# A Mamba-style scan and a mixture of experts on one core: large SBUF tiles moved to multiples of 128 bytes, and the last residual add shared between GpSimd and VectorE

## What is computed

```python
x = x + layernorm(scan(layernorm(x)))      # selective state-space scan, 512 channels x 16 states
x = x + layernorm(moe(layernorm(x)))       # mixture of experts
```

## The kernel before

| tiles | stage | before | changed |
|---|---|---|---|
| `ident` | all | 0 | 0 |
| `xnT` | prepare | 96 | 64 |
| `xpT`, `a_u`, `a_w1`, `a_low`, `a_lg`, `a_dt`, `a_dx` | prepare | 0 | 96 |
| `Bt`, `Ct`, `dts`, `dtxs`, `w1_*`, `w2_*`, `u`, `pr` | mix | 32 | 0 |
| `Xh`, `Xl`, `hhs`, `hls` | mix | 96 | 0 |
| `Xbh`, `Xbl`, `hh`, `hl`, `h32`, `raw`, `xrow`, `yst` | experts | 32 | 0 |
| `Xah`, `Xal`, `Xch`, `Xcl`, `W1h`, `W1l`, `W2h`, `W2l` | experts | 96 | 0 |
| `d_x1*`, `d_y*` | experts, end | 96 | 0 |

## Time and profile before

### The profile page before, as it was taken

One profiled execution on the slowest core, in us unless ns is written; L12 is line 12 of the kernel. 1 busy time (PEld: TensorE's weight loads), 2 busy tenths in 40 slices (PEclk: granted clock), 3 DMA queues, 4 the chain that ended last, 5 costly groups with the idle time before them and its releaser, 6 DMA issues.

```text
span 3578.8 us, 43069 instructions
## 1 busy us (share of the span) xinstructions
PE 3174.4 (89%) x15191; PEld 2574.6 (72%) x15191; DVE 1854.1 (52%) x2708; ACT 1425.5 (40%) x2529; POOL 1732.0 (48%) x1577
## 2 busy tenths in 40 slices
PE   6455699998999987989999999999999999999992
PEld 3233577777777775778888888888888888888881
DVE  6698989998899880552332233222222322222225
ACT  7554676676766762311221322312213213222113
POOL 1187787987888863531440532513415326235102
PEclk8655799999999998979999999999999999999996
DMA  8859688696796946810330421312303214123026
GB/s 258 249 169 243 176 228 221 195 270 185 225 235 201 257 134 183 247 58 19 77 75 9 106 51 42 100 21 71 77 12 98 59 27 109 27 59 83 16 77 229
DMA packets 276920, 463.42 MB, mean 129 GB/s; under 512 B 32065, under 2 KB 107729, under 8 KB 276706
## 3 DMA queue, kind: packets, MB, share of 16 engines
q1 hardware_dynamic: 206656, 266.21, 26.1%
q0 software_dynamic: 68288, 194.06, 20.8%
q10 hardware_dynamic: 1762, 0.40, 0.1%
HBM read 363.44 MB, written 97.14 MB: 129 GB/s over the span
## 4 chain that ended last, share of the span: by engine, by line
PE 55%; DVE 2%; DMA 1%; issue 1%; POOL 1%; ACT 1%; SPq 0%; POOLq 0%; DVEq 0%; ACTq 0%
PE c_psH L1769 27%; PE c_psY L1813 26%; PE c_psT L1760 1%; PE c_psT L1864 1%; DVE d_y L1740 1%; DVE d_st L1724 1%; PE c_psY L1809 0%; DVE yst L1536 0%; DMA xrow<-x_d 0%; DMA raw<-in_w 0%; POOL W1l L1406 0%; DVE hh L1546 0%; ACT h L1320 0%; POOL W2l L1406 0%; DMA acc_d<-yst,sidx 0%
## 5 line engine op out<-in xcount | busy, mean ns | idle before, releaser
L1552 DVE CAST hh<-h 128x512 fp32r<-128x512 f32 (+1 forms) x400 | 176.9, 442 | 1282.3 <-ACT h L1326 1256.5
L826 POOL TENSOR_TENSOR u<-dtxs,Bt 128x512 f32<-128x512 f32 x512 | 670.8, 1348 | 164.2 <-DVE b_psA L729 147.1
L1326 ACT ACTIVATE h<-c_psH,b1e 128x512 f32<-128x512 f32 (+1 forms) x384 | 236.7, 616 | 1281.6 <-PE c_psH L1769 1263.0
L729 DVE TENSOR_TENSOR_SCAN b_psA<-b_psA,carry,u 128x512 f32<-128x512 f32 x512 | 657.0, 1283 | 59.8 <-ACT b_psA L599 56.7
L1813 PE MATMUL c_psY<-W2h,hh 128*128 128x512 f32 x1344 | 540.9, 402 | 0.3
L934 PE MATMUL b_psY<-ident,pr 128*128 128x128 f32 x2048 | 350.4, 310 | 210.6 <-DVE pr L736 192.3
L1813 PE MATMUL c_psY<-W2l,hh 128*128 128x512 f32 x1344 | 531.9, 396 | 0.0
L1813 PE MATMUL c_psY<-W2h,hl 128*128 128x512 f32 x1344 | 531.5, 395 | 0.0
L1411 POOL DMA_INDIRECT xrow<-xt_d,idx x80 | 92.3, 1153 | 852.7 <-PE c_psT L1760 444.9
L934 PEld LDWEIGHTS b_psY<-ident,pr 128*128 128x128 f32 x2048 | 268.7, 158 | 296.4 <-DVE pr L736 243.2
L736 DVE TENSOR_TENSOR pr<-b_psA,Ct 128x512 f32<-128x512 f32 x512 | 354.2, 692 | 19.5 <-DMA Ct<-bc_d 1.8
(11 more groups left out here) (261 smaller groups left out, 5852.9 us busy)
## 6 DMA issues: line engine op xcount, KB each, us to landing
w<-ws_d POOLq DMA_DIRECT2D x224, 512.0 KB, 6.6
raw<-in_w SPq DMA_DIRECT2D x256, 256.0 KB, 2.7
Bt<-bc_d SPq DMA_DIRECT2D x64, 512.0 KB, 14.6
Ct<-bc_d SPq DMA_DIRECT2D x64, 512.0 KB, 19.0
xn<-in_x SPq DMA_DIRECT2D x8, 1024.0 KB, 7.8
xT_d<-xnT SPq DMA_DIRECT2D x8, 1024.0 KB, 8.7
dt_d<-a_dt SPq DMA_DIRECT2D x8, 1024.0 KB, 8.1
dtx_d<-a_dx SPq DMA_DIRECT2D x8, 1024.0 KB, 8.2
```

The source lines that it names most:

```text
L729: nc.vector.tensor_tensor_scan(psA[q][:, :], psA[q][:, :], u[g % U_RING][:, :], carry[:, k:k + 1], ALU.mult, ALU.add).then_inc(s_h, 1)
L826: nc.gpsimd.tensor_tensor(u[g % U_RING][:, :], dtx[s % 2][:, :], Bt[n // TG][:, n % TG, :], ALU.mult)\
L1326: nc.scalar.activation(h32[:, 0:n * P], psH[j % 2][:, 0:n * P], ACT.Gelu, bias=b1[:, j - 1:j]).then_inc(s_gelu, 1)
```

## The change

Two things. First, small tiles are put together: `eps` becomes the first column of a row of 32 float32 (`LINE`, 128 bytes); in `mix` eleven small tiles become slices of one tile `b_few` that is declared behind all large ones; in `experts` `b1T` and `b1e` become one tile of 640 bytes, `slot_g` and `slot_s` another one of 640, and `idx`, `sidx`, `wsl` slices of one tile of 128 bytes. With that the large tiles of `mix` and `experts` start at multiples of 128 bytes. Second, at the end GpSimd adds the residual of the first tile of each pair and VectorE that of the second; GpSimd then waits for both and issues the store. (`slots` becomes `slots_known`, a name alone.)

```diff
+LINE = 32
...
-        carry = sb("carry", [P, NU])
         ys = two("ys", [P, CT, D])
-        st, mv, st2 = sb("b_st", [P, CT, 6]), sb("b_mv", [P, CT, 2]), sb("b_st2", [P, CT, 6])
-        sd, rstd, nmr = sb("b_sd", [P, CT]), sb("b_rstd", [P, CT]), sb("b_nmr", [P, CT])
-        sd2, rstd2, nmr2 = sb("b_sd2", [P, CT]), sb("b_rstd2", [P, CT]), sb("b_nmr2", [P, CT])
-        half = sb("b_minus_half", [P, CT])
         xn = two("xn2_", [P, D])
...
-        b1T, b2bc = sb("sb1T", [P, FC]), sb("sb2bc", [P, D])
+        b2bc = sb("sb2bc", [P, D])
         yst = two("ysh", [P, D]) + xn
+        few = sb("b_few", [P, NU + FC + 14 * CT + 7 * CT])
+        carry, b1T = few[:, 0:NU], few[:, NU:NU + FC]
...
-        b1T = sb("b1T", [P, (E + 1) * FC])
-        b1e = sb("b1e", [P, FC])
-        slot_g, slot_s = sb("slot_g", [P, E * ST]), sb("slot_s", [P, E * ST])
-        idx, sidx = sb("idx", [P, ST], I32), sb("sidx", [P, ST], I32)
-        wsl = sb("slot_weights", [P, ST])
+        biases = sb("biases", [P, (E + 2) * FC])
+        b1T, b1e = biases[:, 0:(E + 1) * FC], biases[:, (E + 1) * FC:(E + 2) * FC]
+        slots = sb("slot_rows", [P, 2, E * ST])
+        slot_g, slot_s = slots[:, 0, :], slots[:, 1, :]
+        few = sb("slot_lists", [P, LINE])
+        idx, sidx = few[:, 0:ST].bitcast(I32), few[:, ST:2 * ST].bitcast(I32)
+        wsl = few[:, 2 * ST:3 * ST]
...
             for g in range(NT // TAIL_G):
-                pool.wait_ge(d_x, (g + 1) * TAIL_G)
+                pool.wait_ge(d_x1[g], 16)
+                pool.wait_ge(d_n, g * TAIL_G + 1)
+                nc.gpsimd.tensor_tensor(y[g][:, 0, :], y[g][:, 0, :], x1r[g][:, 0, :], ALU.add).then_inc(d_xp, 1)
+                pool.wait_ge(d_xp, g + 1)
+                pool.wait_ge(d_x, g + 1)
                 nc.gpsimd.dma_start(tail_rows(out_d, g), y[g][:, :, :]).then_inc(d_out, 16)
...
             def residual(g):
                 dve.wait_ge(d_x1[g], 16)
-                for t in range(TAIL_G):
-                    dve.wait_ge(d_n, g * TAIL_G + t + 1)
-                    v.tensor_tensor(y[g][:, t, :], y[g][:, t, :], x1r[g][:, t, :], ALU.add).then_inc(d_x, 1)
+                dve.wait_ge(d_n, (g + 1) * TAIL_G)
+                v.tensor_tensor(y[g][:, 1, :], y[g][:, 1, :], x1r[g][:, 1, :], ALU.add).then_inc(d_x, 1)
...
-            ("ident", [P, P], F32), ("eps", [P, 1], F32), ("mv_x1", [P, NT, 2], F32))}
+            ("ident", [P, P], F32), ("eps_row", [P, LINE], F32), ("mv_x1", [P, NT, 2], F32))}
+        const["eps"] = const["eps_row"][:, 0:1]
```

More of the change, by code:

```diff
@@ L408, in mix @@
         g0, hh0 = sb("g0", [P, CH]), sb("b_low_h", [L3, CH], F32R)
-        b1T, b2bc = sb("sb1T", [P, FC]), sb("sb2bc", [P, D])
+        b2bc = sb("sb2bc", [P, D])
         yst = two("ysh", [P, D]) + xn
+        few = sb("b_few", [P, NU + FC + 14 * CT + 7 * CT])
+        carry, b1T = few[:, 0:NU], few[:, NU:NU + FC]
+        st, st2 = (few[:, NU + FC + i * 6 * CT:NU + FC + (i + 1) * 6 * CT].rearrange("p (t n) -> p t n", t=CT)
+                   for i in range(2))
+        mv = few[:, NU + FC + 12 * CT:NU + FC + 14 * CT].rearrange("p (t n) -> p t n", t=CT)
+        sd, rstd, nmr, sd2, rstd2, nmr2, half = (
+            few[:, NU + FC + (14 + i) * CT:NU + FC + (15 + i) * CT] for i in range(7))
         psA = [ctx.enter_context(nc.psum_tensor(f"b_psA{q}", [P, CH], F32)) for q in range(2)]
@@ L1117, in experts @@
         d_y, d_x1 = ([sem(f"d_{n}{g}") for g in range(NT // TAIL_G)] for n in ("sum_in", "x1_in"))
-        d_out = sem("d_stored")
+        d_out, d_xp = sem("d_stored"), sem("d_x2_first")
         d_st, d_mv, d_sd, d_rs, d_nm, d_n, d_x = (
@@ L1414, in gather, with slots_known @@
                     bounds_check=T - 1).then_inc(s_xg[t % 2], 16)
-            def slots(e):
+            def slots_known(e):
                 pass_gate(pool, s_idx, e + 1, g_pool)
@@ L1488, in _ @@
                 pool.wait_ge(s_xts[q], BT // 2 * 16)
-            slots(0)
+            slots_known(0)
             gathers(0, 0, range(2))
@@ L1503, in steady @@
                 if not last:
-                    slots(e + 1)
+                    slots_known(e + 1)
                     gathers(e + 1, 0, range(2))
```

## The result

The changed kernel takes 3592.32 us (median of 20 runs, 3587.1 to 3598.95), the kernel before 3585.15 us beside it (20 runs, 3580.03 to 3590.53). The ratio is 1.0019, with a 95% interval of 1.0012 to 1.0025: 7 us slower, where 150 us less were predicted. The profiled execution took 3592.35 us, its span 3590.6 us.

A forecast was written before the change was run, and what follows sets the result against it. TensorE's matmul pace was taken to bound experts, VectorE the scan in mix and the end pairs; -131 - 4.5 - 18 + 3 = -150 us against 3580.5 gave 3430, with 2.3 for the median 3432 us, range 3395 to 3545.

The forecast's parts named there:

- The pace (-131 us): Experts' split products on TensorE: operands on multiples of 128 bytes lose most of each matmul's surplus, 131 us less.
- rival A: Split products: the operands' offsets against each other count, all go to about 226 ns; experts -43 us, total 3535; chance 0.15.
- Rival B: Split products: multiple of 128 does not matter, surplus is a fixed cost of changing stationary columns; 3575 to 3590; chance 0.11.
- Rival C: End part: pace stays, GpSimd add, VectorE add and store exclude each other for longer, 3.4 us a pair; 3592; chance 0.08.
- Mix (-18 and -4.5 us): Split products in mix: 18 us less before 1321 us through VectorE's waits for ScalarE, 4.5 us less after it.
- Other engines at nothing: VectorE's operations neither gain nor lose by tile placement; DMAs and ScalarE cost nothing, 3 us either way.
- The last residual (+3 us, measured +7): End part: one residual add of each pair moved to GpSimd, excluding VectorE's two-input operations; +3 us, ends -8 and +7.
- The sum of 2.97 us: End part, one pair: GpSimd's add, small VectorE operation, rest of VectorE's add, wait and store; 0.1 us more than now.
- the last two stores: End of the kernel: they come at the pair chain's pace instead of 2.14 and 1.20 us, about +1.5 us.
- VectorE's add with a mean above 1 us: End part: sign that the forecast is right, VectorE's residual add being held by GpSimd's; 0.69 us would show no meeting.

The follow-up runs named there:

- equal_at_0: Changed kernel with slot_lists moved into free columns of eps_row, so experts' split-product operands (one group a block excepted) start equal modulo 256; 3559.96 us, 0.9928 of before.
- align_only: Changed kernel with its tile placement kept but both residual adds back on VectorE; 3583.49 us, ratio 0.9994 to the kernel before.
- nm_one_input: Changed kernel with VectorE's minus mean times rstd made by two one-SBUF-input tensor_scalar instructions instead of one two-input scalar_tensor_tensor; 3590.96 us, ratio 1.0014 to before.

## Why the prediction was wrong

- **The pace (-131 us), the step that failed.** "A row of 2048 or 1024 bytes that starts off a multiple of 128 touches one piece of 128 bytes more" was inferred from a surplus of 13 ns at both widths. The runs show those 13.3 ns at every place, multiples of 128 included, for 512, 384 and 320 columns. They come with float32r (bfloat16: 2.5 ns) at a granted clock of 1.00, and no placement removed them. The experts kept their pace: TensorE was busy for 2036.8 us of the stretch where the forecast had 131 less. What placement does move is the other 0 to 7.7 ns, by the distance of the two operands modulo 256. The target of 216 ns was taken from plain float32 products at two clocks a column; it is the pace of bfloat16 here.
- **What was overlooked.** The observation that "the pace goes with the offsets" was right, and so was rival A's thought that the operands count against each other. But the table was drawn modulo 128, the unit of the change. Modulo 256 it would have shown 96 for `W1`, `W2`, `Xa` and 160 for `Xb`, `hh`; the row with both equal was the fast one, and the changed kernel puts them at 128 and 0. Rival A then priced the change as if all became equal: 43 us, where equal_at_0 gained 26 against the kernel before, 33 without the 7 that the end part costs; the change itself does not do that. Its other reason, that equal offsets and the best pace coincide, was right.
- **Rivals B and C.** The outcome, 7 us against the kernel before, is between them. Rival B had the pace unchanged and +3 us for the end, 3575 to 3590; the measured 3592 is just outside. Its premise, that placement does not matter and the surplus is a fixed cost of changing the stationary operand, is refuted by the distances (27 us) and by the row with the same stationary operand; a cost of each weight load, changed or not, could be behind the remaining 13.3 ns and was not tried. Rival C, with a chance of 0.08, had the direction, the place (the chain through GpSimd's queue) and the very number, 3592. The number is luck in part: it was +9 on 3583, where +7 on 3585 were measured. It came from GpSimd's add held up to 1.83 us and 14 times 0.55 us; the trace has that add at 1.27 us in every pair, 0.34 us more a pair, and twice the price that C put on the last stores. The Trainium skill's rule of 16-byte cachelines ("SBUF — State Buffer", "Specifications (TRN2)") was read as "all tiles are aligned already", which led close to the right time for a wrong reason: starts at multiples of 32 bytes differ by up to 7.7 ns a matmul. No run here shows such lines, though a shift by 16 bytes does change the pace.
- **The rule of the Trainium skill on the pace** ("TensorE: Matmul & The Clock Gate", "Wait — 56ns, not 53.3ns?"), N/2.4 + 2.5 ns, agrees with the bfloat16 rows (215.8 and 109.2 ns) and not with float32r (226.7 at best). Reading the whole of its distance from the trace as something that the layout costs was the error; up to 7.7 ns of it are.
- **Mix (-18 and -4.5 us).** The matmuls of mix did get distance 0: the full groups of `up` went from 240.2 to 236.9 ns, those of `down` from 236.7 to 236.4. That is about 5 us of TensorE's time, not 37, and VectorE's waits for ScalarE did not shrink (61.0 us). align_only at a ratio of 0.9994 (0.9985 to 1.0003) shows no gain clear of noise.
- **Other engines at nothing**: held. In the stretch of experts VectorE, ScalarE and GpSimd are busy for 625.4, 505.5 and 695.9 us, before for 628.9, 505.0 and 697.0.
- **The last residual (+3 us, measured +7).** The mechanism was right: two-input operations of VectorE and GpSimd's add stand still for one another, and a store stands ahead of the next add. The term was mis-sized, in two places. The sum of 2.97 us had VectorE's add end 0.08 + 0.55 = 0.63 us behind GpSimd's, and that is what was measured (3551.37 - 3550.74). But it had the store go out 0.30 us later, as in the earlier trace rows, and measured are 0.56, here and in nm_one_input (why was not tried). That makes 3.22 us instead of 2.97, 0.34 more than before: 13 times 0.34 is 4.4 us, where 1.3 were summed. And the last two stores were priced at +1.5. They go out (kernel before, then changed) at

```profile
3568.37 0.73 POOL L1522 DMA_DIRECT2D out<-d_y  x1 [2.14 <-DVE d_y L1740]
3570.51 0.72 POOL L1522 DMA_DIRECT2D out<-d_y  x1 [1.40 <-DVE d_y L1740]
3571.71 0.72 POOL L1522 DMA_DIRECT2D out<-d_y  x1 [0.48 <-DVE d_y L1740]
...
3577.62 0.72 POOL L1531 DMA_DIRECT2D out<-d_y  x1 [1.19 <-ACT d_y L1399]
3580.83 0.73 POOL L1531 DMA_DIRECT2D out<-d_y  x1 [1.19 <-ACT d_y L1399]
3583.97 0.72 POOL L1531 DMA_DIRECT2D out<-d_y  x1 [1.12 <-DVE d_y L1748]
```

3.21 and 3.14 us apart where they were 2.14 and 1.20, which adds 3.0. That makes 7.4; 7.5 were measured from the first statistics to the last store. The sign "VectorE's add with a mean above 1 us" did not come, since `d_nm` stands ahead of that add and is held in its place (adds 0.68 us, median). The Trainium skill's rule ("SBUF — State Buffer", "Who interferes with whom") agrees, whatever the size of the operation: one on 2 elements a partition is held for the whole 1.11 us, and the tensor_scalar with one tensor input is not.

## What to carry to other kernels

Where TensorE is the bound with float32r operands, compare the starts of stationary and moving tiles modulo 256 in the built program, against each other rather than against a boundary; making them equal was worth 27 us of 3585 here and costs a pad. A table of offsets should be drawn for several moduli before a rule is read from it, and a rule for a pace is cheap to try on a row of matmuls alone. When an add is moved to a queue that also stores, issue the add ahead of the older store: the same shared add lost 7 us behind it and won 6 ahead of it.

## What was not expected of the hardware

- Float32r matmuls of 512 columns come every 226.7 ns at best at a granted clock of 1.00, 13.3 ns above their columns, and every 228.9 to 234.6 when the two operands' starts differ in most other ways modulo 256. What lies behind it stays open; the 13.3 ns too. At a granted clock of 0.50 they are gone (426.7 ns).
- Neither VectorE, ScalarE, GpSimd nor 292 GB/s of DMA traffic changed that pace (232.4 ns, at distance 128) by more than 0.2 ns.
- The intervals repeat in short cycles that belong to the distance, e.g. 226, 227, 227 at 0, or 236, 231 at 64. A group that begins after a turn takes up to ten matmuls to fall into its cycle.
- 128 moving columns take 111.7 ns in float32r, 58 above their columns, and 192 take the same.
- An operation of VectorE on 2 elements a partition with two tensors in SBUF is held for 1.11 us by GpSimd's add of 128 x 512; with one tensor it is not (0.33 us for two).
